# Sums and values of a head group in one PSUM bank and two bursts, raw scores over three banks: a change in the attention stage of an early-fusion transformer block

## The reference

```
q, k, v = x Wq, x Wk, x Wv            # 16 heads of 32, 4 key/value heads, rotary on q and k
scores  = q k^T * 32**-0.5
attn    = softmax(scores)             # over 384 keys
out     = (attn v) Wo ;  h = h + out
h = h + experts(layernorm(h))         # top 6 of 64, plus a shared expert
```

## Time and profile before

| | us |
|---|---|
| median of 3 runs | 1477.85 (1473.19 to 1486.64) |
| the profiled execution | 1462.84 |
| its span, first to last instruction | 1461.0 |
| TensorE matmul busy | 1267.7 (87%) |
| VectorE busy | 759.0 (52%) |
| ScalarE busy | 420.8 (29%) |
| GpSimd busy | 501.3 (34%) |

### The profile page before, as it was taken

One profiled execution on the slowest core, in us unless ns is written; L12 is line 12 of the kernel. 1 busy time (PEld: TensorE's weight loads), 2 busy tenths in 40 slices (PEclk: granted clock), 3 DMA queues, 4 the chain that ended last, 5 costly groups with the idle time before them and its releaser, 6 DMA issues. The chain is left out here.

```text
span 1461.0 us, 23472 instructions
## 1 busy us (share of the span) xinstructions
PE 1267.7 (87%) x9192; PEld 819.4 (56%) x9192; DVE 759.0 (52%) x1667; ACT 420.8 (29%) x695; POOL 501.3 (34%) x453
## 2 busy tenths in 40 slices
PE   5197578889898999989888879999999999999995
PEld 5196434344546464636444768756666656666662
DVE  6984466757676868676866352323222222232221
ACT  2211223444435354444445421111111111111110
POOL 0000101011203434343467376243444444444345
PEclk9698769999999999999999889999999999999998
DMA  3023141321505152524243384799999999998983
GB/s 114 0 60 94 30 103 41 77 50 43 142 17 146 42 131 63 128 66 107 66 137 118 118 291 74 212 309 300 330 304 302 318 337 329 282 362 290 325 267 44
DMA packets 139829, 239.82 MB, mean 164 GB/s; under 512 B 61112, under 2 KB 81224, under 8 KB 139720
## 3 DMA queue, kind: packets, MB, share of 16 engines
q1 hardware_dynamic: 115880, 214.10, 46.0%
q0 software_dynamic: 23840, 24.23, 9.2%
HBM read 175.59 MB, written 38.90 MB: 147 GB/s over the span
## 5 line engine op out<-in xcount | busy, mean ns | idle before, releaser
L1969 POOL DMA_INDIRECT out_rows<-mo_y,mo_scatter_half x128 | 182.1, 1423 | 244.2 <-DMA out_rows<-mo_y,mo_scatter_half 172.3
L1332 DVE TENSOR_REDUCE at_maxes<-at_ps 128x1 f32<-128x384 f32 x384 | 195.1, 551 | 63.2 <-PE at_ps L894 57.3
L1100 ACT ACTIVATE bulk<-at_ps 128x1152 f32<-128x1152 f32 x128 | 144.5, 1129 | 263.4 <-PE at_ps L861 262.3
L1592 POOL DMA_INDIRECT slot_table<-at_toki,at_si x144 | 143.3, 995 | 105.4 <-DVE at_maxes L1332 76.1
L70 PE MATMUL mo_ps<-arena_view,arena_view 128*117 128x384 f32 (+1 forms) x864 | 168.8, 344 | 1.1 <-PEq L549 1.1
L70 PEld LDWEIGHTS mo_ps<-arena_view,arena_view 128*117 128x117 f32 (+1 forms) x864 | 146.6, 179 | 14.6 <-issue 14.5
L894 PE MATMUL at_ps<-late_view,late_view 128*128 128x384 bf16 x384 | 116.7, 354 | 35.8 <-DVE at_maxes L1332 18.0
L852 PE MATMUL at_ps<-arena_view,arena_view 128*128 128x512 f32 (+1 forms) x576 | 114.8, 350 | 3.8 <-ACT arena_view L1185 2.4
L894 PEld LDWEIGHTS at_ps<-late_view,late_view 128*128 128x128 bf16 x384 | 31.2, 98 | 145.7 <-DVE at_maxes L1332 111.7
L852 PEld LDWEIGHTS at_ps<-arena_view,arena_view 128*128 128x128 f32 x576 | 90.3, 193 | 36.6 <-issue 22.3
L861 PE MATMUL at_ps<-arena_view 97*128 97x384 f32 x384 | 97.6, 363 | 9.2 <-DMA arena_view<-at_mrow 5.1
(11 more groups left out here) (218 smaller groups left out, 1820.5 us busy)
## 6 DMA issues: line engine op xcount, KB each, us to landing
bulk<-in_L_ffn_w_gate SPq DMA_DIRECT2D x32, 704.0 KB, 7.4
bulk<-in_L_ffn_w_up SPq DMA_DIRECT2D x32, 704.0 KB, 8.9
late_view<-in_L_ffn_w_gate SPq DMA_DIRECT2D x32, 704.0 KB, 7.5
late_view<-in_L_ffn_w_up SPq DMA_DIRECT2D x32, 704.0 KB, 9.2
arena_view<-arena_view SPq DMA_DIRECT2D x96, 192.0 KB
late_view<-in_L_ffn_w_down SPq DMA_DIRECT2D x32, 512.0 KB, 6.1
bulk<-in_L_ffn_w_down SPq DMA_DIRECT2D x32, 512.0 KB, 6.4
out_rows<-at_hr SPq DMA_DIRECT2D x8, 768.0 KB, 3.8
```

What stands on the lines that cost most here:

```text
L1100: A.activation(PT[:, N % RING, :, :], ps[:, 0:NT, 0:SEQ], ACT.Exp, scale=float(HD) ** -0.5)\
L1332: V.tensor_reduce(maxes[:, half, s, h:h + 1], ps[:, raw_bank(a, u), 0:SEQ], AX.X, ALU.max, negate=True)\
L1592: G.indirect_dma_start(slot_table, bass.IndirectOffsetOnAxis(ap=si[:, e % 2, m:m + 1], axis=0), toki[:, e % 2, m // TOPK:m // TOPK + 1], N ...
L1969: G.indirect_dma_start(acc_halves, bass.IndirectOffsetOnAxis(ap=scatter_half[:, half, 2 * p + e:2 * p + e + 1], axis=0), y[:, p % 2, e, co ...
```

## The change

Sums and values of a group both go to bank 3. Steps 0 to 2 (sums) are issued in one burst in the first slot of the next group, steps 3 to 5 (values) in one burst in the third; the second and fourth slot have none. The burst of sums waits for the division of the group before, the burst of values for the first transpose of the inversion, which frees the bank. On VectorE the inversion moves to the second of the four slots, behind its first two maxima, and the division to the fourth. Raw scores rotate over banks 4, 5 and 6, and a unit waits for the maximum three units back instead of two; the second half of the first sequence keeps its two banks. On SP the loads of the shared gate and up weights in the last iteration no longer wait for the stacked heads; that wait and the first load of shared rows move behind the store of the turned rows. Behind the loop VectorE does the last inversion ahead of the residual add and statistics. The new name `AHEAD_UNITS` equals `UNITS`, so that the number of raw units in each slot stays the same.

```diff
-        VALUE_STEPS = {0: (0, 1), 1: (2, 3), 2: (4,), 3: (5,)}
+        VALUE_STEPS = {0: (0, 1, 2), 1: (), 2: (3, 4, 5), 3: ()}
...
+        AHEAD_UNITS = UNITS
+
         def raw_units(b, n):
...
-            if -1 <= b < B - 1 and n >= RAW_FROM and (b >= 0 or n < RAW_FROM + REP):
-                return b + 1, range(PER_SLOT * (n - RAW_FROM), PER_SLOT * (n - RAW_FROM + 1))
+            if b == -1 and RAW_FROM <= n < RAW_FROM + REP:
+                return 0, range(PER_SLOT * (n - RAW_FROM), PER_SLOT * (n - RAW_FROM + 1))
+            if 0 <= b < B - 1 and n >= RAW_FROM:
+                return b + 1, range(AHEAD_UNITS * (n - RAW_FROM) // (NH - RAW_FROM),
+                                    AHEAD_UNITS * (n - RAW_FROM + 1) // (NH - RAW_FROM))
...
         def raw_bank(a, u):
-            return (7, 4)[u % 2] if a == 0 and u >= HALF_UNITS else 5 + u % 2
+            if a == 0 and u >= HALF_UNITS:
+                return (7, 4)[u % 2]
+            return 4 + u % 3
...
             def load_shared_weights():
-                for done, count in ((q_ready, NT), (kv_ready, NT), (heads_turned, NTILE), (qb_ready, NTILE),
-                                    (stacked[0], STACK), (stacked[1], STACK)):
+                for done, count in ((q_ready, NT), (kv_ready, NT), (heads_turned, NTILE), (qb_ready, NTILE)):
                     sp.wait_ge(done, count * B)
...
-                sp.wait_ge(x2T_stored, 16 * (B - 3))
-                shared_rows_in(0)
...
                 if prev2:
                     store_turned(d)
+                if b == B - 1:
+                    for done in stacked:
+                        sp.wait_ge(done, STACK * B)
+                    sp.wait_ge(x2T_stored, 16 * (B - 3))
+                    shared_rows_in(0)
+                if prev2:
                     store_rows(d)
...
                 if q == 0:
                     pe.wait_ge(probs_ready, REP * (G + 1))
-                    wait(pe, divide_step, DIVIDE_STEPS * (G - 1) + 1 if G else 0)
-                    wait(pe, max_ready, 0 if G else UNITS)
+                    wait(pe, o_ready, G)
                 if q == NT:
                     pe.wait_ge(v_copied, NT * (b + 1))
-                    wait(pe, o_ready, G)
+                    pe.wait_ge(divide_step, DIVIDE_STEPS * G + 1)
                 for j in range(REP):
                     w = ones[:, :] if sums else vv[:, b % 3, kt, HD * g:HD * (g + 1)]
-                    m = T.matmul(ps[HD * j:HD * (j + 1), 3 + sums, 0:SEQ], w, PT[:, (REP * G + j) % RING, kt, :],
+                    m = T.matmul(ps[HD * j:HD * (j + 1), 3, 0:SEQ], w, PT[:, (REP * G + j) % RING, kt, :],
...
-                if u < 2:
+                if u < 3:
                     pe.wait_ge(qlo_ready, NTILE * (a + 1))
-                wait(pe, max_ready, UNITS * a + u - 1)
+                if a > 0 or u < HALF_UNITS:
+                    wait(pe, max_ready, UNITS * a + max(u - 2, 0))
+                else:
+                    wait(pe, max_ready, u - 1)
...
-                    for q in steps[0:1]:
+                    for q in steps:
                         values(G, q)
...
-                    for q in steps[1:2]:
-                        values(G, q)
...
-                link(V.transpose(sT, ps[:, 4, 0:SEQ]), divide_step)
+                link(V.transpose(sT, ps[:, 3, 0:SEQ]), divide_step)
...
-                    if n % REP == 0:
-                        divide(NKV * b + n // REP - 2)
+                    if n % REP == 1:
+                        invert_sums(NKV * b + n // REP - 1)
+                    if n % REP == REP - 1:
+                        divide(NKV * b + n // REP - 1)
...
-                    if n % REP == REP - 2:
-                        invert_sums(NKV * b + n // REP - 1)
...
-            divide(NKV * B - 2)
+            invert_sums(NKV * B - 1)
             residual(B - 2, NT - 1)
             statistics2(B - 2)
-            invert_sums(NKV * B - 1)
             divide(NKV * B - 1)
```

More of the change, by code:

```diff
@@ L899, in turn_x @@
                     pe.wait_ge(xn_ready, NT * (a + 1))
-                    wait(pe, max_ready, HALF_UNITS if a == 1 else UNITS * a)
+                    wait(pe, max_ready, HALF_UNITS if a == 1 else UNITS * (a - 1) + AHEAD_UNITS)
                 if k >= 2:
@@ L1624, in _ @@
                         for m in range(first, last):
-                            pool.wait_ge(max_ready, UNITS * a + 1 + UNITS * m // SCATTERS)
+                            pool.wait_ge(max_ready, UNITS * a + 1 + AHEAD_UNITS * m // SCATTERS)
                             scatter(e, m, m + 1)
```

## The result

The changed kernel takes 1509.64 us (median of 4 runs, 1505.88 to 1524.28) against 1477.16 for the kernel before beside it (4 runs, 1473.19 to 1486.64): the ratio is 1.0229, 95% interval 1.0145 to 1.0313. It is slower by 32.5 us, where +12 was forecast; the time lies 1.6 us above the range. The profiled execution of after took 1507.67 us with a span of 1505.9; that of before, 1462.84, turned out to be a short one: two more profiles of the same kernel had spans of 1470.5 and 1481.2. The profiled execution of experiment e8 was a disturbed one, and only its ratio is read.

A forecast was written before the change was run, and what follows sets the result against it. The prediction took TensorE and VectorE as nearly full in slots 8 to 15 and a chain over SP and VectorE as ending last in slots 0 to 7; its terms summed to +12 on 1477.85, forecasting 1490 us, range 1466 to 1508.

The forecast's parts named there:

- the walk: Slots 8 to 15, new order timed with profiled prices: stops in slots 9, 11, 13; next sequence at 36.45 us, before 35.25.
- The sum: Whole kernel: -1.5 + 1.7 + 5 x (1.2 + 0.9) + 1.8 = +12 us (12.5).
- Slots 8 to 15: Third to seventh sequence, first raw score to next sequence: 1.2 us added each, new waits in slots without values.
- The clock rival: Attention stage: one more low-clock stretch of 1.7 us in each of seven sequences, +12 on top, 1502 us; chance 0.22.
- Slots 0 to 7: Third to seventh sequence: first raw score 0.9 us later, 0.43 from the burst between token transposes plus 0.5 on VectorE.
- the inversion's new place: Slots 0 to 7, VectorE: inversion earlier and one division more, 0.5 us; other waits covered, else up to 1 us a sequence.
- The last sequence: Loop's end and tail: residual's store and the loads behind it on SP late by 1.96 + 1.48 - 1.6 = 1.8 us.
- the late residual: Behind the loop: residual add waits for the last sums (1.96 us) and the inversion (1.48) now ahead of it.
- the 1.6 us set against it: Last sequence: loop's end estimated 1.6 us earlier, eight removed steps at 0.2 each.
- First sequence: Slots 8 to 15 about 31.4 us instead of 33.2, slots 0 to 7 give some 0.3 back: -1.5 us.
- The third bank pays: Rival, attention stage: the 15.2 us of raw-score waits go, some -10 to -15 us, at the most 1463; chance 0.15.
- Drained switches: Rival, TensorE: each switch drains a pipeline, so removed steps save 4.8 instead of 0.8 in slots 8 to 15; 1462; chance 0.08.

The follow-up runs named there:

- e8: Kernel before with the steps in bursts in slots 8 to 15 only: 1513.77 us, ratio 1.0201 to the kernel before.
- e4: Changed kernel plus unused matmuls into a free bank, 8 ahead of slot 7's head transposes, 14 ahead of the first raw score: 1501.6 us, ratio 1.0131.
- e7: Kernel before with the steps in bursts in slots 0 to 7 only: 1490.33 us, ratio 1.0076.
- e1: Kernel before with the bursts alone, keeping its banks and its old places on VectorE and SP: 1514.0 us, ratio 1.0234.
- e6: Kernel before with three raw banks and one bank for sums and values only for groups of slots 8 to 15, steps spread: 1472.77 us, ratio 0.9937.
- e13: Like the kernel before, but slots 8 to 15 have three raw banks, one sums/values bank, bursts and the change's inversion and division places: 1497.08 us, ratio 1.0112.
- e2: Changed kernel with its banks, but steps spread again and inversion and division moved to the end of their slots: 1490.08 us, ratio 1.0101.
- e14: Changed kernel with GpSimd's scatters (indirect DMAs) of the last sequence three slots later: 1523.17 us, ratio 1.0308.

## Why the prediction was wrong

**The sign and the stops of the walk were right, terms of the sum were mis-sized or missing.** The sum had +12, the profiles show +41 and the timed runs +32.5. Beyond the forecast the profiles have 8.7 us in slots 0 to 7 of the third to seventh sequence, 8.3 in their slots 8 to 15, 7.1 in the last sequence, 2.9 in the first and 1.5 in the second.

**Slots 8 to 15: +2.85 a sequence instead of +1.2.** Most of the walk held. Slot 11 was to take 4.38 us and takes 4.37 to 4.39 in the third to seventh sequence; slots 12 to 15 were to take 18.23 and take 18.2 to 18.6 in four of these five, with the stops in 9, 11 and 13 named ahead. In the fifth, slot 12 too ran partly at the low clock (6.7 us instead of 5.1; granted 0.50 from 587.1 to 590.3). The step that failed is slot 8, behind the stops at the head transposes: the burst was priced at the full clock in the one slot where the clock was not full. By the walk the three raw scores behind it go 2.53 us after raw score 0; in the fifth sequence they go 3.84 after it (567.03 to 570.87), and raw score 11 of slot 9, which the walk has at 7.84, goes at 9.12 (576.15), as much later. The fifth sequence was also a poor baseline: slot 8 of before takes 4.4 us in it, but 5.4 to 5.9 in nine of the fifteen sequences of three profiles, with part of the low stretch in it. Against the mean of before (36.18) the walk's 36.45 was +0.3, and it is 2.6 short.

**A wait that the walk did not have, in slots 10 and 14.** Behind the burst of values the first maximum starts 1.09 us after its raw score (580.05, 581.14) instead of 0.38, and slot 10 takes 5.6 us instead of 5.1. This is so in 15 of the 16 slots 10 and 14 of the fourth to seventh sequence in the two profiles of after, each time beside a scatter of GpSimd (here 579.72 to 580.69); the second and third sequence have no scatters and no such delay. Most maxima beside a scatter are on time, and before has two late ones in three profiles, so the cause is open.

**The clock rival came true on top of the forecast.** The prediction had priced it so, as +12 more, but gave it a chance of 0.22 and no place in the sum. Between the first scores of the first and of the last sequence TensorE was granted the lower level for 36.1, 32.0 and 31.9 us in the three profiles of before and for 69.3 and 72.8 in after. e4 has 38.3, about as little as before, and with it gets back some 7 us of the profile and 8 of the median: rather less than 12, and by the timed runs not clear of the spread. The range, up to 1508, held forecast and rival together (1502); what took the time beyond it lies mostly in the next two terms.

**Slots 0 to 7: +2.63 instead of +0.9.** The residual add came as forecast, 0.53 us later from the sequence's start (5.52 against 4.99). In the fifth sequence so did the statistics, 0.39 later (24.37 against 23.98), forecast 0.43; but over the third to sixth sequence of all profiles they come 1.05 later (25.32 against 24.27), as the tokens arrive later by more than the residual does, which I did not trace. The step that failed is the next one, the inversion's new place, taken at nothing beside 0.5 us for a division: I counted VectorE's list up to the last low part of the queries, so that an inversion moved forward within it cancelled. But TensorE and GpSimd leave that list in the middle. In the fifth sequence the last rotary products are 1.41 us later from the start (35.17 against 33.76), and with them the rotary sum and the head transposes (37.50 against 36.09); the 1.5 us saved behind them become a wait (1.73 at 564.98). That is the 1.8 us of the fifth sequence. In the mean of the third to sixth the products come 1.2 us later behind the statistics (10.8 against 9.6), and the first raw score another 0.5 behind them, which stays open. e7 and e1, with the bursts but the old place, have +1.0; e6 and e13, with the old steps and the old place of the inversion there, have 0.5 and 0.2. No run moves the inversion alone.

**The last sequence: +8.9 instead of +1.8.** Of the term, the late residual came as forecast:

```profile
835.96 2.14 PE L888 MATMUL at_ps<-bulk,at_ones 128*32 128x384 f32 x24
838.17 0.58 DVE L1358 STREAM_TRANSPOSE arena_view<-at_ps 128x384 f32<-128x384 f32 x1 [3.40 <-PE at_ps L888]
...
839.67 0.69 DVE L1374 TENSOR_TENSOR at_hr<-at_hr,at_ps 128x512 f32<-128x512 f32 x1
```

It stands 3.7 us behind the start of the last sums, where before it came at their side. What failed is the 1.6 us set against it, the earlier end of the loop: the last sums begin 64.45 us behind the first scores of the sequence (mean), 59.28 in before, so 5.2 later. Slot 4 has some 3 of these: 10.7 and 9.4 us, against 5.1, 8.1 and 7.6; there the logits fall into stops whose cause is open, and which in before stand behind the logits or are absent. The one profile of before that the prediction rests on had none of these stops in that sequence. The remaining 2 us are spread over the other slots, and I did not trace them.

**First sequence, +1.4 instead of -1.5.** The third bank's gain of 1.8 us there needs spread steps: from the first raw score it is 30.8 us in e6 and 30.7 in e2, 35.3 in after, 33.1 in before.

**The other rivals.** The third bank pays, in e6, by 0.6%; in bursts it does not pay for them. Drained switches are out: the burst at the full clock takes 2.07 us, as priced (2.1), and eight removed switches made no slot shorter than the walk had it. What SP's order in the last sequence costs is not shown, as no run changes it alone. From the last residual add of the loop to the first gate load it is 40.2 to 40.6 us in all five profiles of before and after, so that nothing is lost there; e1, with the old order and the old tail, has a last sequence of 101.6 us, within the 95.3 to 103.5 of before.

## What to carry to other kernels

Interleaved small steps were worth more here than the switches they cost, as two engines exchange buffers: a burst starves the one, and the slots without it starve the other. An operation moved forward in an engine's list is not free because the list's total is unchanged; ask which other engines take something from the middle of it. And before a stretch of one sequence serves as the baseline and its prices as the full clock's, compare it with the same stretch of its neighbours, and read the granted clock at the very place where work is to be put.

## What the runs showed of the hardware that was not expected

TensorE can stand for microseconds with nothing to wait for that the profile shows: in the last sequence its matmuls and weight loads came one by one some 0.7 us apart (764.64 and 765.35 above), in four of the five profiles of both kernels. In e14, with GpSimd's indirect DMAs moved away, there was none of it at the logits; but in before such DMAs run beside the logits without it, and in the earlier sequences they run in slots 8 to 15, where no such series of stops stands. Why it happens is open. One profile of a kernel can lie 5 to 8 us under others of the same kernel in one stage, here the last sequence, while the third to seventh sequence agree from profile to profile within 1.4 us in before and 2.4 in after.
